# Reordering the first ten groups of a relational graph layer on every engine

## What is computed

```python
h = maximum(layernorm(x), 0)                       # mean and variance over the 128 features of a node
hw = h @ W_loop.T ;  g = hw @ Wg_loop.T
vals = (hw + b_loop) * sigmoid(g + bg_loop)
out = x + relu(einsum('bnm,bmd->bnd', swap(adj) == 1, vals) + the same for relations 2 to 40)
```

## Time and profile before

| | |
|---|---|
| three runs | 107.48, 107.17, 106.65 us; median 107.17 |
| profiled execution | 107.37 us, span of its instructions 105.6 us |
| busy in the span | PE 97.2 us (92%), DVE 93.1 (88%), ACT 88.9 (84%), POOL 82.3 (78%) |
| DMA | 25.48 MB, 240 GB/s of memory traffic over the span |

### The profile page before, as it was taken

One profiled execution on the slowest core, in us unless ns is written; L12 is line 12 of the kernel. 1 busy time (PEld: TensorE's weight loads), 2 busy tenths in 40 slices (PEclk: granted clock), 3 DMA queues, 4 the chain that ended last, 5 costly groups with the idle time before them and its releaser, 6 DMA issues. The chain is left out here.

```text
span 105.6 us, 2484 instructions
## 1 busy us (share of the span) xinstructions
PE 97.2 (92%) x796; PEld 91.8 (87%) x796; DVE 93.1 (88%) x204; ACT 88.9 (84%) x144; POOL 82.3 (78%) x154
## 2 busy tenths in 40 slices
PE   5999897897999999997999999979999999999960
PEld 2358795896999999996999999979999999999950
DVE  1289499999999999999999999999999998878780
ACT  4155659899899989997999899997999899999840
POOL 2288959999998999599989996999989999970000
PEclk9999999999999999999999999999999999999999
DMA  2899999999999999999999999997606070606077
GB/s 69 243 315 291 291 289 291 289 291 295 292 300 304 314 343 325 287 283 321 317 316 323 337 328 325 338 321 219 173 6 199 0 199 0 205 6 199 0 206 204
DMA packets 50275, 25.48 MB, mean 241 GB/s; under 512 B 850, under 2 KB 50260, under 8 KB 50260
## 3 DMA queue, kind: packets, MB, share of 16 engines
q1 hardware_dynamic: 49984, 25.17, 86.4%
q10 hardware_dynamic: 276, 0.13, 0.5%
HBM read 16.91 MB, written 8.39 MB: 240 GB/s over the span
## 5 line engine op out<-in xcount | busy, mean ns | idle before, releaser
L329 POOL TENSOR_SCALAR xn<-x_all,mean_neg,rstd 128x128 f32<-128x128 f32 x92 | 40.8, 454 | 1.9 <-issue 1.3
L724 PE MATMUL psum<-w_hi,hT_hi 128*128 128x256 f32 x128 | 34.3, 302 | 0.7 <-ACT psum L396 0.4
L746 PE MATMUL psum<-vals,mask 128*128 128x128 f32 x256 | 33.6, 275 | 0.8 <-DVE vals L523 0.8
L396 ACT ACTIVATE psum<-bias_all 128x1024 f32<-128x1024 f32 x32 | 33.0, 1030 | 0.8 <-DVE vals L523 0.8
L746 PEld LDWEIGHTS psum<-vals,mask 128*128 128x128 f32 x256 | 31.0, 191 | 0.9 <-issue 0.9
L725 PE MATMUL psum<-w_lo,hT_hi 128*128 128x256 f32 x128 | 31.4, 280 | 0.0
L490 DVE BATCH_NORM_STATS2 stats<-x_all 128x6 f32<-128x256 f32 x64 | 24.0, 419 | 3.7 <-DMA x_all<-in_x 3.7
L724 PEld LDWEIGHTS psum<-w_hi,hT_hi 128*128 128x128 f32 x128 | 24.5, 191 | 1.5 <-issue 0.9
L523 DVE TENSOR_TENSOR vals<-psum,gate 128x512 f32<-128x512 f32 (+1 forms) x33 | 21.9, 662 | 4.2 <-ACT gate L411 3.9
L314 POOL TENSOR_TENSOR rstd<-var_eps,minus_half 128x16 f32<-128x16 f32 (+2 forms) x11 | 24.3, 2213 | 0.9
L725 PEld LDWEIGHTS psum<-w_lo,hT_hi 128*128 128x128 f32 x128 | 24.6, 192 | 0.0
(11 more groups left out here) (35 smaller groups left out, 31.8 us busy)
## 6 DMA issues: line engine op xcount, KB each, us to landing
adj_all<-in_adj SPq DMA_DIRECT2D x16, 512.0 KB, 7.1
x_all<-in_x SPq DMA_DIRECT2D x15, 512.0 KB, 6.7
out<-x_all SPq DMA_DIRECT2D x15, 512.0 KB, 6.0
x_all<-in_x SPq DMA_DIRECT2D x2, 256.0 KB, 3.1
out<-x_all SPq DMA_DIRECT2D x1, 256.0 KB, 2.6
out<-x_all ACTq DMA_DIRECT2D x1, 128.0 KB, 2.8
out<-x_all SPq DMA_DIRECT2D x1, 128.0 KB, 2.9
w_raw<-in_L_gnn_W_loop SPq DMA_DIRECT2D x1, 64.0 KB, 2.4
```

The lines of the kernel that those rows point to most:

```text
L329: last = pool.tensor_scalar(xn[:, g % XN, j * D:j * D + D], x_all[:, g * GC + j * D:g * GC + j * D + D], mean_neg[:, b % BATCH_SLOTS, k:k ...
L396: nc.scalar.activation(prod_ps[s].rearrange("p g a d -> p g (a d)"), bias_all[:, :, :].rearrange("p a d -> p (a d)").unsqueeze(1) .to_broa ...
L724: nc.tensor.matmul(to, hi, w_hi[:, :], start=False, stop=False, skip_group_check=True)
L746: last = nc.tensor.matmul(to[:, j * D:j * D + D], mask[:, g % MASKS, j * N:j * N + N], vals[:, s, j * D:j * D + D], start=True, stop=True)
```

## The change

- **Shares.** Of groups 0 to 5, groups 0 and 3 are normalised by VectorE alone and 1, 2, 4 and 5 by GpSimd alone; before it was 1 graph by GpSimd for groups 0 and 1 and 3 for the others. From group 6 on nothing changes.
- **VectorE's prologue.** The statistics of groups 3 to 9 stand at other places among `messages`, `low_part` and `output`.
- **GpSimd.** Minus the mean is made ahead of the power, not behind it, in all batches (and not at all for batch 0). The masks of groups 2 and 3 go to ScalarE.
- **ScalarE.** It issues the two weight DMAs, which SP issued before. It waits first for a new semaphore `bias_cleared`, since its bias DMAs now write into a tile of 128 rows that VectorE clears. `seed(2)`, `relu_turned(2)` and `sigmoid(1)` go ahead of masks. `watch` runs later by four steps: the first is in step 4, and chunks 13, 14 and 15 are at the end.
- **SP.** `x` of chunk 3 goes ahead of `adj` of chunk 0, and so on: each `adj` chunk one place later.
- **TensorE.** Four more multiplications by zeros, and the bias row is spread by a matmul over 128 rows where it was one.

```diff
+    POOL_SHARES = (0, 4, 4, 0, 4, 4)
+    WATCH_LAG = 4
...
         def pool_share(g):
-            return 1 if g < 2 else 3
+            return POOL_SHARES[g] if g < len(POOL_SHARES) else 3
...
         def mask_by_act(g):
-            return g < 2 or g % MASKS == MASKS - 1
+            return g < 4 or g % MASKS == MASKS - 1
...
             load_tile(x_all, x, 0, 0, GROUP, x_first)
-            sp.dma_start(w_raw[:, 0, :], W_loop).then_inc(w_loaded, 16)
-            sp.dma_start(w_raw[:, 1, :], Wg_loop).then_inc(w_loaded, 16)
             load_tile(x_all, x, GROUP, GC, CG - GROUP, x_loaded[0])
             load_x(1)
             load_x(2)
+            load_x(3)
             load_adj(0)
-            for c in range(3, LOAD_AHEAD):
+            for c in range(4, LOAD_AHEAD):
                 load_x(c)
-                load_adj(c - 2)
+                load_adj(c - 3)
...
                 pool.tensor_scalar(var_eps[:, s, 0:n].rearrange("p (k e) -> p k e", e=2), st[:, :, :, 2],
                                    1.0 / D, EPS, ALU.mult, ALU.add).then_inc(var_ready, 1)
+                if means_before(b + 1) > means_before(b):
+                    pool.tensor_scalar(mean_neg[:, s, 0:n].rearrange("p (k e) -> p k e", e=2), st[:, :, :, 1],
+                                       -1.0, 0.0, ALU.mult, ALU.add).then_inc(mean_ready, 1)
                 pool.wait_ge(var_ready, b + 1)
                 pool.tensor_tensor(rstd[:, s, 0:n], var_eps[:, s, 0:n], minus_half[:, 0:n], ALU.pow
                                    ).then_inc(rstd_ready, 1)
-                pool.tensor_scalar(mean_neg[:, s, 0:n].rearrange("p (k e) -> p k e", e=2), st[:, :, :, 1],
-                                   -1.0, 0.0, ALU.mult, ALU.add).then_inc(mean_ready, 1)
...
             coefficients(0)
-            normalise(0)
             coefficients(1)
             normalise(1)
             coefficients(2)
             normalise(2)
-            normalise(3)
-            for t in range(GROUPS):
+            coefficients(3)
+            normalise(4)
+            normalise(5)
+            for t in range(2, GROUPS):
...
             act.preload_act_table(ACT.Sigmoid)
+            act.wait_ge(bias_cleared, 1)
             act.dma_start(bias_row[0:1, 0, :], b_loop).then_inc(bias_loaded, 16)
             act.dma_start(bias_row[0:1, 1, :], bg_loop).then_inc(bias_loaded, 16)
+            act.dma_start(w_raw[:, 0, :], W_loop).then_inc(w_loaded, 16)
+            act.dma_start(w_raw[:, 1, :], Wg_loop).then_inc(w_loaded, 16)
...
             sigmoid(0)
             relu_turned(1)
             edges(0)
+            seed(2)
+            relu_turned(2)
+            sigmoid(1)
             edges(1)
+            edges(2)
             act.wait_ge(half_ready, 1)
-            for t in range(GROUPS):
+            for t in range(1, GROUPS - 1):
                 if live(t + 2):
                     relu_turned(t + 2)
                     seed(t + 2)
-                if live(t + 1):
-                    sigmoid(t + 1)
-                if t % CHUNK == 0:
-                    watch(t // CHUNK)
+                sigmoid(t + 1)
+                if WATCH_LAG <= t < GROUPS - 2 and t % CHUNK == 0:
+                    watch((t - WATCH_LAG) // CHUNK)
                 if live(t + 2) and mask_by_act(t + 2):
                     edges(t + 2)
+                if t == GROUPS - 3:
+                    watch(CHUNKS - 3)
+            watch(CHUNKS - 2)
             act.wait_ge(half_out, 1)
             act.dma_start(
...
+            watch(CHUNKS - 1)
...
             normalise(0)
             split_weights(0)
             row_stats(2)
+            row_stats(3)
             split_weights(1)
-            row_stats(3)
             low_part(0)
-            normalise(1)
+            row_stats(4)
+            row_stats(5)
+            row_stats(6)
             messages(0)
             low_part(1)
-            normalise(2)
-            row_stats(4)
-            row_stats(5)
+            row_stats(7)
             normalise(3)
             low_part(2)
-            row_stats(6)
-            row_stats(7)
+            messages(1)
             row_stats(8)
-            for t in range(1, GROUPS + 1):
+            output(0)
+            low_part(3)
+            row_stats(9)
+            for t in range(2, GROUPS + 1):
                 if live(t):
                     messages(t)
                 output(t - 1)
-                if live(t + 3):
+                if live(t + 3) and pool_share(t + 3) < GROUP:
                     normalise(t + 3)
...
-            keep_busy(3, 1)
+            keep_busy(5, 1)
             pe.wait_ge(ones_ready, 1)
+            pe.wait_ge(bias_cleared, 1)
             pe.wait_ge(bias_loaded, 32)
-            nc.tensor.matmul(bank[7][:, 256:512], ones[0:1, :], bias_row[:, :, :].rearrange("p a d -> p (a d)"),
+            nc.tensor.matmul(bank[7][:, 256:512], ones[:, :], bias_row[:, :, :].rearrange("p a d -> p (a d)"),
                              start=True, stop=True).then_inc(bias_spread, 1)
             pe.wait_ge(ident_step, 2)
             pe.wait_ge(w_loaded, 32)
-            turn_weights(w_raw[:, 0, :], w_raw[:, 1, :], w_gT[:, :], w_turned, w_gT_ready, 1, 2)
-            keep_busy(3, 1)
+            turn_weights(w_raw[:, 0, :], w_raw[:, 1, :], w_gT[:, :], w_turned, w_gT_ready, 1, 3)
+            keep_busy(4, 1)
```

More of the change, by code:

```diff
@@ L67, in build @@
         zeros = sb("zeros", [128, 4 * D], BF16)
-        bias_row = sb("bias_row", [1, 2, D])
+        bias_row = sb("bias_row", [128, 2, D])
         junk = sb("junk", [128, 2, CC], BF16)
@@ L87, in build @@
         w_loaded = sem("w_loaded")
+        bias_cleared = sem("bias_cleared")
         bias_loaded = sem("bias_loaded")
@@ L203, in pool_share, with pool_groups, dve_groups, means_before @@
         def pool_share(g):
-            return 1 if g < 2 else 3
+            return POOL_SHARES[g] if g < len(POOL_SHARES) else 3
+        def pool_groups(g):
+            return sum(pool_share(k) > 0 for k in range(g))
+        def dve_groups(g):
+            return sum(pool_share(k) < GROUP for k in range(g))
+        def means_before(b):
+            return sum(any(pool_share(g) for g in range(BATCHES[k][0], BATCHES[k][1] + 1)) for k in range(b))
         def mask_by_act(g):
-            return g < 2 or g % MASKS == MASKS - 1
+            return g < 4 or g % MASKS == MASKS - 1
         def masks_before(g, by_act):
@@ L245, in _ @@
             load_x(2)
+            load_x(3)
             load_adj(0)
-            for c in range(3, LOAD_AHEAD):
+            for c in range(4, LOAD_AHEAD):
                 load_x(c)
-                load_adj(c - 2)
+                load_adj(c - 3)
             for c in range(LOAD_AHEAD, CHUNKS):
                 load_x(c)
-                load_adj(c - 2)
+                load_adj(c - 3)
                 sp.wait_ge(out_ready, (c - LOAD_AHEAD + 1) * CHUNK)
                 store_tile((c - LOAD_AHEAD) * CG, (c - LOAD_AHEAD) * CC, CG)
+            load_adj(CHUNKS - 3)
             load_adj(CHUNKS - 2)
@@ L322, in normalise @@
                 if g == first:
+                    pool.wait_ge(mean_ready, means_before(b + 1))
                     pool.wait_ge(rstd_ready, b + 1)
-                    pool.wait_ge(mean_ready, b + 1)
                 if g >= XN:
@@ L477, in _ @@
             nc.vector.memset(zeros[:, :], 0.0).then_inc(zeros_ready, 1)
+            nc.vector.memset(bias_row[:, :, :], 0.0).then_inc(bias_cleared, 1)
             nc.vector.memset(ones[:, :], 1.0).then_inc(ones_ready, 1)
@@ L487, in row_stats @@
                 if g == first and b >= BATCH_SLOTS:
-                    dve.wait_ge(mean_ready, b - BATCH_SLOTS + 1)
+                    dve.wait_ge(rstd_ready, b - BATCH_SLOTS + 1)
+                    dve.wait_ge(mean_ready, means_before(b - BATCH_SLOTS + 1))
                 for j in range(0, GROUP, 2):
@@ L498, in normalise @@
                 b, first, _ = batch_of(g)
-                if g == first:
+                if dve_groups(g) == dve_groups(first):
                     dve.wait_ge(rstd_ready, b + 1)
@@ L700, in _ @@
             pe.wait_ge(w_loaded, 32)
-            turn_weights(w_raw[:, 0, :], w_raw[:, 1, :], w_gT[:, :], w_turned, w_gT_ready, 1, 2)
-            keep_busy(3, 1)
+            turn_weights(w_raw[:, 0, :], w_raw[:, 1, :], w_gT[:, :], w_turned, w_gT_ready, 1, 3)
+            keep_busy(4, 1)
             def turn_rows(g):
                 s = g % 2
-                pe.wait_ge(normed_pool, g + 1)
-                pe.wait_ge(normed_dve, g + 1)
+                if pool_share(g) > 0:
+                    pe.wait_ge(normed_pool, pool_groups(g + 1))
+                if pool_share(g) < GROUP:
+                    pe.wait_ge(normed_dve, dve_groups(g + 1))
                 if g >= 2:
```

2 lines of the change are left out of this document (1 added, 1 removed).

## The result

| | before | after |
|---|---|---|
| median of the runs | 107.03 us (106.65 to 107.48, four runs) | 110.48 us (109.03 to 111.17, four runs) |
| profiled execution, span | 107.37, 105.6 us | 110.93, 109.1 us |
| granted clock, mean | 1.00 | 0.957 |

The four executions of the change took 109.03, 110.03, 110.93 and 111.17 us, with a mean granted clock of 1.00, 0.979, 0.957 and 0.969; the profiled one is that of 110.93. The ratio is 1.0217, 95% interval 1.0150 to 1.0283, and leaves out the two with the lowest clock, though the low clock is part of the effect here: in the profiled execution it lies between 7 and 15 us, behind a stop of TensorE. Even the execution that reads full clock is 2.0 us over the median before. By the medians of all runs the change is slower by 3.4 us, by the ratio by 2.3, where 0.9 us gained was forecast and the range ended at 107.6.

What follows compares the result with a forecast made beforehand. VectorE's batch statistics plus a 5.15 us chain to TensorE's transposes were taken to set the time. Terms 0.9 + 0.2 + 0.35 - 0.55 = 0.9 us gained: 107.37 becomes 106.5, median said as 106.2, range 104.9 to 107.6.

Steps and rivals of the forecast that it cites:

- Term 1: Start: weights issued at 2.65 take 3.2 us, land 0.9 us late; first low part at 10.2 instead of 9.29.
- the far bound: Weight landing at the start: at most 6.7 us, as a chunk takes behind others.
- "slower" rival: Start: weights queue 5.2 us, first low part 12.2, kernel 108.3 us; at the full 6.7, 109.8; chance 0.10.
- Term 2: VectorE from first low part to group 2's messages: 9.8 us instead of 11.6; 0.9 us gained including the late start.
- "I take no difference" on the clock: TensorE's start: clock rises as before, keeping 2.47 and 1.75 us; a rise behind group 0's products would cost 0.6.
- an early rise: TensorE's start: clock up before the weights come would shrink the 2.47 and 1.75 us by up to 1.0 together.
- Term 3: GpSimd's batch chain: mean ahead of the power saves 0.17 us once, counted as 0.2 us gained.
- Term 4: Middle, groups 6 to 22: two blocked tiles as before, 0.35 us gained, between 1.6 gained and 0.2 lost.
- Term 5: Tail: a `watch` ahead of group 31's sigmoids loses 0.55 us; two later `watch` lie under the last DMAs.
- The rival in which the order does nothing: Prologue: VectorE only swaps waits, terms 1, 4 and 5 remain, 107.5 us; chance 0.20 together with late weights.

Runs made afterwards that it cites:

- experiment 2: Kernel before with only the two weight loads issued by ScalarE behind its bias loads: 109.58 us, ratio 1.0217.
- experiment 3: Changed kernel with ScalarE issuing the weight loads first, ahead of the wait and the bias loads: 108.63 us, ratio 1.0131.
- experiment 1: Changed kernel with both weight loads back on SP's queue, behind the first quarter of x: 107.6 us, ratio 1.0038.
- experiment 4: Changed kernel with 16 more TensorE multiplications by zeros ahead of the wait for the weights: 108.74 us, ratio 1.0134.
- experiment 5: Changed kernel with weights on SP's queue and `watch` in the steps where the kernel before has it: 107.62 us, ratio 1.0031.
- experiment 7: Kernel before with only the mean moved ahead of the power in every batch: 108.3 us, ratio 1.0110.
- experiment 6: Changed kernel with weights on SP's queue and the mean again behind the power: 108.23 us, ratio 1.0099.
- experiment 10: Changed kernel, weights on SP's queue, `watch` two groups late, VectorE's tile behind the low part up to step 26: 106.65 us, ratio 0.9950.
- 11: Kernel before with only VectorE's tile moved behind the low part in all steps but the last four: 107.61 us, ratio 1.0035.
- 12: As experiment 10, with an extra `watch` in step 15 and each from step 16 where the kernel before has it: 106.17 us, ratio 0.9913.

## Why the prediction was wrong

**Term 1 is the step that failed,** and in it the sentence "I take 3.2, that of the same transfer". The value came from a load that stood in SP's queue behind the first 256 KB of `x` alone, ahead of all other loads. Issued 0.9 us later and on another queue, the same 64 KB took 5.5 us, close to the 6.7 of a chunk, the far bound that I had named. The "slower" rival has this mechanism: at 5.2 us it gave the low part at 12.2 and 108.3; measured are 5.5 and 12.56, and a median 2.2 us above its 108.3. I had given it too little chance, because "64 KB isn't 512 KB" and because of the Trainium skill (DMA: Bandwidth & Descriptors, "Queues, rings and completion order"), by which each DMA engine takes turns between queues. No run here contradicts turns as such, but the conclusion that the weights therefore don't wait was wrong: 5.5 and 5.4 us (the change, experiment 2) against 2.7 on SP's queue. Issued first on ScalarE's queue they took 3.1 and 4.0 (experiment 3), so when they are issued matters more than their size; what the other queue itself adds the runs don't part.

The miss against the profiled execution is 4.4 us (106.5 forecast, 110.93 measured). Read at the marks it is 2.4 at the first low part, all of it the landing, 0.5 in term 2, 0.1 from there to group 6, 0.4 in the middle, 0.6 behind group 22 and 0.4 between the last output and the end.

**"I take no difference" on the clock** held where the sum uses it: the 2.47 and 1.75 us from turning the weights to the first low part came out as 4.20, at the same lower level as before. Behind it the 0.6 us that I kept as a bound was enough: from the first low part to the first messages it is 3.23 us instead of 2.93. What I hadn't priced is what the wait throws away. The change's multiplications bring TensorE to its upper level before the weights come (experiment 1); with a wait of 3.16 us instead of nearly 1 it is back at 0.50, and zeros in the wait bring the first low part 1.55 us sooner (experiment 4). The Trainium skill (TensorE: Matmul & The Clock Gate, "Part 1") says that the clock falls back after idleness, which is what the table of stretches shows; I had written that it speaks against the gap. That an early rise could be worth up to 1.0 us wasn't so in this order: experiment 1 has it and its first low part is at 9.61, since TensorE then waits for group 0's tiles, which I had held to be ready well ahead of it.

**Term 2 had the mechanism and most of the size.** From the first low part to group 2's messages I had said 9.8 us instead of 11.6. It is 10.3 in the change, 10.05 in experiment 1 and 9.5 in experiment 4; six statistics instructions do cover the wait of the earlier trace rows, which is 0.52 us in the change and nothing in 1. That the late `watch` has 0.7 of it, by leaving ScalarE free, I hadn't seen (experiment 5).

**Term 3** was 0.17 us. It measured 0.09 in the change, 0.27 in the kernel before (experiment 7), and nothing between experiments 1 and 6. Its side effect was larger: in the kernel before, the shift of the casts by some 0.2 us brought a long tile in every batch (experiment 7).

**Term 4** had the mechanism and not the number. I took two long tiles as before, within bounds of none to three from group 6 to 22. It was one in each batch: three, the worst bound, and they took back the 0.25 us that step 2 saves without a tile (distance of the transposes 45.15 us against 45.10). Behind group 22 there are two where the kernel before has one. I had put nothing there; the marks show +0.62 us, about one long tile. Once in step, the pattern repeats: the next batch starts when VectorE's statistics are ready, so the casts come at the same distance from VectorE's tile again. Experiment 10, which takes the tile out of their way, is worth 1.0 us. What decides whether a program falls into step is open: moving the mean brought it about in the kernel before (experiment 7), moving it back in the changed one didn't end it (experiment 6).

**Term 5** was right to 0.01 us for the sigmoids (0.56 measured, 0.55 said) and wrong for "the two `watch` that come later lie under the last DMAs". I counted 3.2 us from the flag to the end of the span as cover. But some 1.9 us of these are the branch behind the flag (107.21 to 109.1), which moves with it. From VectorE's last output to the end of the span it is 3.2 to 3.3 us where the flag comes with the outputs (before, experiments 2, 5, 7, 11, 12), and 3.7 to 3.9 where a `watch` stands behind the output DMA (the change and all other experiments).

With the landing put right, and with it the clock, experiment 1 measured 107.6 us: the order is then no gain either, since terms 4 and 5 and the flag give back what term 2 brings.

Two sums on the side don't come out. The rival in which the order does nothing leaves terms 1, 4 and 5: 0.9 and 0.55 lost and 0.35 gained give 108.3, not 107.5. And term 4's better bound is 0.35 + 1.0, 1.35 gained, not 1.6. Neither enters the forecast.

## What to carry to other kernels

A load that something early waits for belongs ahead of the bulk loads in issue order; moving it to an idle queue doesn't move it ahead of what is already under way, so cost it at the bulk's time until a run shows better. A long wait of TensorE early in a kernel can cost more than its length, if it had reached its upper level: here the work behind the wait ran at the lower one, and zeros multiplied meanwhile brought the first low part 1.55 us sooner. Read the level from the durations of like matmuls too, since the printed clock missed it at the start of the kernel before. When two engines run at nearly one pace, look at which instructions stand beside each other in every period: one tile moved behind its neighbour was worth 1.0 us here, about as much as the whole order of the prologue (1.2 us at group 6), and only the two kernels with both (experiments 10 and 12) beat the one before, by 0.5% and, with an early flag too, 0.9%.

## What was unexpected of the hardware

- Two 64 KB loads on a second queue, issued 0.5 us behind each other at 2.3 and 2.7 us beside SP's stream, took 4.5 and 5.5 us, and 3.1 and 4.0 issued first on it; on SP's own queue 2.4 to 3.3.
- A VectorE tile from SBUF to SBUF (128x128, 0.33 us) stays until GpSimd's int32 casts end, when these begin up to 0.34 us behind it: 0.82, 0.90 and, with two casts, 1.58 us. The statistics beside casts kept their 0.75 to 0.77 us a pair. The Trainium skill (GPSIMD Engine Reference, "1. Specifications") says that the SBUF interfaces are shared for some VectorE forms; the traces agree and add the size.
- In the change some 1.8 us pass from the flag to the end of the span, with VectorE's last output done 1.8 us before the flag.
